# Heads' projection of a transformer layer: the turn by position moved from VectorE into each token's weights, keys and queries in the two row halves of TensorE's array

## What is computed

```python
h = _rmsnorm(x, ln1_w)
q = (h @ wq.T).reshape(Bx, Tx, NH, HD).transpose(0, 2, 1, 3)
k = (h @ wk.T).reshape(Bx, Tx, NKV, HD).transpose(0, 2, 1, 3)
v = (h @ wv.T).reshape(Bx, Tx, NKV, HD).transpose(0, 2, 1, 3)
q = q * cos + _rotate_half(q) * sin          # cos, sin: a row for each position
k = k * cos + _rotate_half(k) * sin
k, v = jnp.repeat(k, NREP, axis=1), jnp.repeat(v, NREP, axis=1)
scores = jnp.einsum('bhtd,bhsd->bhts', q, k) / jnp.sqrt(jnp.float32(HD))
```

## Time and profile before

| | |
|---|---|
| three runs | median 1144.41 us (1140.83 to 1145.59) |
| the profiled execution | 1143.9 us, its span in the trace 1142.1 us |
| mean granted TensorE clock | 0.965 of 2.4 GHz |
| busy share of the span: PE, PEld, DVE, ACT, POOL | 91%, 67%, 76%, 52%, 39% |
| heads' projection (project1) | 587.2 to 652.5 us |
| heads (heads1) after it | from 653.3 us |

### The profile page before, as it was taken

How to read it: one execution, slowest core, us unless ns; L and a number is a source line. 1 busy time by engine, 2 the same in 40 slices (tenths; PEclk the granted TensorE clock), 3 DMA queues, 4 the chain that set the end, 5 groups by cost and what they waited for, 6 DMA issues and landing times. The chain is left out here.

```text
span 1142.1 us, 24219 instructions
## 1 busy us (share of the span) xinstructions
PE 1038.3 (91%) x8559; PEld 765.1 (67%) x8559; DVE 865.5 (76%) x2076; ACT 598.7 (52%) x1293; POOL 449.5 (39%) x599
## 2 busy tenths in 40 slices
PE   6697868589999999998889899986999999999996
PEld 2376756467777777776765467764777777777775
DVE  1696969757777777778878689965788887787876
ACT  2275646465556555666334457764554545545542
POOL 3233402303444344434357377724133333333332
PEclk9798999889999999999899999997999999999999
DMA  8200000000000000000000000000000000000000
GB/s 231 119 1 1 3 1 2 1 1 2 1 2 1 2 1 1 1 1 1 1 1 1 1 1 3 3 2 0 2 6 7 7 7 13 7 6 7 7 7 13
DMA packets 3456, 13.59 MB, mean 12 GB/s; under 512 B 400, under 2 KB 2192, under 8 KB 2960
## 3 DMA queue, kind: packets, MB, share of 16 engines
q1 hardware_dynamic: 3056, 8.00, 2.5%
q0 software_dynamic: 288, 4.11, 0.9%
HBM read 9.98 MB, written 2.13 MB: 11 GB/s over the span
## 5 line engine op out<-in xcount | busy, mean ns | idle before, releaser
L1461 PE MATMUL moe_psU<-moe_nT_parts,moe_w_hi 128*128 128x320 f32 x988 | 325.0, 339 | 3.4 <-DVE moe_hid L1356 2.5
L1461 PE MATMUL moe_psU<-moe_nT_parts,moe_w_lo 128*128 128x320 f32 x988 | 297.0, 311 | 0.0
L1461 PEld LDWEIGHTS moe_psU<-moe_nT_parts,moe_w_hi 128*128 128x128 f32 x988 | 188.3, 191 | 58.4 <-issue 50.1
L1461 PEld LDWEIGHTS moe_psU<-moe_nT_parts,moe_w_lo 128*128 128x128 f32 x988 | 188.9, 191 | 0.0
L1350 DVE TENSOR_TENSOR moe_hid<-moe_psU,moe_silu 128x320 f32<-128x320 f32 x286 | 139.3, 491 | 57.6 <-ACT moe_silu L1123 49.3
L1033 POOL TENSOR_TENSOR moe_sum<-moe_scaled 128x256 f32<-128x256 f32 x124 | 94.9, 765 | 163.4 <-DVE moe_scaled L1340 163.2
L1123 ACT ACTIVATE moe_silu<-moe_psU 128x320 f32<-128x320 f32 x286 | 125.4, 438 | 57.3 <-PE moe_psU L1461 45.0
L1128 ACT ACTIVATE moe_hid<-moe_psU,middle 128x320 f32<-128x320 f32 x260 | 129.3, 526 | 32.1 <-PE moe_psU L1461 30.0
L1356 DVE TENSOR_SCALAR moe_hid<-moe_psU,middle 128x320 f32<-128x320 f32 x156 | 85.5, 549 | 56.5 <-PE moe_psU L1461 55.5
L1472 PE MATMUL moe_psY<-moe_hid,late 128*64 128x320 f32 x832 | 123.5, 439 | 0.8 <-DVE moe_hid L1350 0.8
L1472 PE MATMUL moe_psY<-moe_hid,middle 128*64 128x320 f32 x832 | 123.5, 439 | 0.7 <-ACT moe_hid L1128 0.7
(11 more groups left out here) (322 smaller groups left out, 1887.6 us busy)
## 6 DMA issues: line engine op xcount, KB each, us to landing
images<-in_x SPq DMA_DIRECT2D x8, 576.0 KB, 11.5
late<-in_late POOLq DMA_DIRECT2D x1, 2456.5 KB, 12.1
out_tokens<-h SPq DMA_DIRECT2D x13, 160.0 KB, 1.8
middle<-in_middle POOLq DMA_DIRECT2D x1, 1554.0 KB, 7.0
early<-in_early SPq DMA_DIRECT2D x1, 1043.0 KB, 19.2
early<-in_early SPq DMA_DIRECT2D x1, 80.0 KB, 2.0
```

The source lines that it names most:

```text
L1461: last = pe.matmul(psum[:, 0:HALF], w[:, col:col + SPLIT], moving, start=(part == 0), stop=(part == 1))
```

## The change

It leaves out `product`, `rotate` and `fold`, and with them VectorE's and GpSimd's part in keys and queries.

- A table "turns" (128 x 65 x 64 floats, 2.1 MB) holds for each position the 16 x 16 matrix that turns a head, once for each head, with 1/4 in those for the queries. Its first group is loaded in the tokenizer, after late; the others by SP in project1, into three buffers, each once the weights' product that used the buffer is done.
- `turned_weights(g)` is one product of 320 columns with wqk (128 x 128, keys in the upper half, queries in the lower), which gives each of the five tokens' own weights: rows 0 to 63 for keys, 64 to 127 for queries. ScalarE copies them (`weights`) into one of two turned_w buffers, 16 columns of every 32; the others are zeroed once by GpSimd.
- normalise writes each token twice, side by side, so that the transposes give nT in both row halves, 128 rows.
- `keys_and_queries(g)` on TensorE is ten products of 64 rows by 128 columns, five tokens in the upper row half into psK, and five in the lower into psQ, in turn. ScalarE copies psK and psQ into kx and qx.
- The values side has a PSUM bank of its own (psV); its ScalarE copy no longer waits for the next transposes.

TensorE's order is now keys and queries of g, values side of g, transposes of g + 1, weights of g + 1. The prediction calls these KQ, side, T and the weights' product. ScalarE's is transposed of g + 1, weights of g + 1, square of g + 3, keys and queries of g, sides of g.

```diff
+def twice_over(dve, dst, src, per_token):
+
+    shape = [B, T, 2, D]
+    return dve.tensor_tensor(dst[:, :, :].rearrange("b t (x d) -> b t x d", x=2), src[:, :, :].unsqueeze(2).to_broadcast(shape),
+                             per_token.unsqueeze(2).unsqueeze(3).to_broadcast(shape), ALU.mult)
...
+                pool.dma_start(turns_first[:, :, :], dram_turns[:, 0:T, :]).then_inc(late_in, 16)
...
-        n_tile, k_parts = [n_first, sb("n_tile1", [B, T, D])], [sb(f"k_parts{k}", [128, TOK]) for k in range(2)]
-        psT, psQ, psK, psF = ps("psT", 128, TOK), ps("psQ", 128, TOK), ps("psK", 128, TOK), ps("psF", 128, TOK)
...
+        n_tile = [n_first, sb("n_tile1", [B, T, 2 * D])]
+        turns = [turns_first] + [sb(f"turns{k}", [128, T, D]) for k in range(2)]
+        turned_w = [sb(f"turned_w{k}", [128, T, 128]) for k in range(2)]
+        psT, psQ, psK = ps("psT", 128, TOK), ps("psQ", 128, TOK), ps("psK", 128, TOK)
+        psW, psV = ps("psW", 128, T * D)[:, 0:T * D], ps("psV", 128, T * B // 4)[:, 0:T * B // 4]
...
+            @block.sync
+            def _(sp):
+                for g in range(1, NT):
+                    need(sp, W_mm, g - 2)
+                    sp.dma_start(turns[g % 3][:, :, :], turns_d[:, g * T:(g + 1) * T, :]).then_inc(turns_in[g % 3], 16)
+
             @block.gpsimd
             def _(pool):
                 pool.memset(halves[:, :], -0.5).then_inc(half_set, 1)
                 pool.wait_ge(half_set, 1)
+                for w in turned_w:
+                    pool.memset(w[:, :, :], 0.0).then_inc(blank, 1)
+                pool.wait_ge(blank, 2)
                 for g in range(NT):
-                    pool.memset(nT[D:, g * TOK:(g + 1) * TOK], 0.0).then_inc(blank, 1)
-                    pool.wait_ge(blank, g + 1)
...
-                    dve.tensor_tensor(n_tile[g % 2][:, :, :], cen[g % 3][:, :, :], over_width(stats[g % 3][:, 4, :]),
-                                      ALU.mult).then_inc(n_set, 1)
+                    twice_over(dve, n_tile[g % 2], cen[g % 3], stats[g % 3][:, 4, :]).then_inc(n_set, 1)
                     dve.tensor_tensor(x[:, g * T:(g + 1) * T, :], cen[g % 3][:, :, :], over_width(stats[g % 3][:, 3, :]),
                                       ALU.mult).then_inc(x_set, 1)
-
-                def rotate(src, table, g, dst):
-                    angles = late[:, c[table]][:, g * T:(g + 1) * T].unsqueeze(2).to_broadcast([128, T, B])
-                    return dve.tensor_tensor(dst.rearrange("p (t b) -> p t b", b=B),
-                                             src[:, 0:TOK].rearrange("p (t b) -> p t b", b=B), angles, ALU.mult)
-
-                def keys(g):
-                    dve.wait_ge(K_mm, g + 1)
-                    need(dve, F_mm, g - 1)
-                    rotate(psK, "ropek", g, k_parts[g % 2][:, :]).then_inc(k_parts_set, 1)
-
-                def queries(g):
-                    dve.wait_ge(Q_mm, g + 1)
-                    rotate(psQ, "ropeq", g, at(qx, g)).then_inc(q_set, 1)
 
...
                 for g in range(NT):
                     if g < NT - 3:
                         centre(g + 3)
-                    keys(g)
                     if g < NT - 2:
                         normalise(g + 2)
                     if g < NT - 3:
                         variance(g + 3)
-                    queries(g)
 
             @block.scalar
             def _(act):
@@ -1865,31 +1866,37 @@
 
                 def transposed(g):
                     act.wait_ge(T_mm, g + 1)
-                    act.activation(at(nT, g)[0:D, :], psT[0:D, 0:TOK], ACT.Copy, scale=late[0:D, c["ln1"]]).then_inc(nT_set, 1)
-
-                def folded(g):
-                    act.wait_ge(F_mm, g + 1)
-                    act.copy(at(kx, g), psF[:, 0:TOK]).then_inc(k_set, 1)
+                    act.activation(at(nT, g), psT[:, 0:TOK], ACT.Copy, scale=late[:, c["ln1"]]).then_inc(nT_set, 1)
+
+                def weights(g):
+                    act.wait_ge(W_mm, g + 1)
+                    act.wait_ge(blank, 2)
+                    need(act, Q_mm, g - 1)
+                    act.copy(turned_w[g % 2][:, :, :].rearrange("d t (h x i) -> d t h x i", h=NH, x=2)[:, :, :, 0, :],
+                             psW.rearrange("d (t h i) -> d t h i", t=T, h=NH)).then_inc(w_set, 1)
 
                 def keep_sides(g):
                     act.wait_ge(V_mm, g + 1)
-                    if g < NT - 1:
-                        act.wait_ge(T_mm, g + 2)
                     act.copy(sides[:, :, g * T:(g + 1) * T].rearrange("p q t -> p t q"),
-                             side_ps.rearrange("p (t q) -> p t q", t=T)).then_inc(side_set, 1)
-
+                             psV.rearrange("p (t q) -> p t q", t=T)).then_inc(side_set, 1)
+
+                def keys_and_queries(g):
+                    act.wait_ge(Q_mm, g + 1)
+                    act.copy(at(kx, g), psK[:, 0:TOK]).then_inc(k_set, 1)
+                    act.copy(at(qx, g), psQ[:, 0:TOK]).then_inc(q_set, 1)
+
+                transposed(0)
+                weights(0)
                 square(1)
-                transposed(0)
                 square(2)
                 for g in range(NT):
+                    if g < NT - 1:
+                        transposed(g + 1)
+                        weights(g + 1)
                     if g < NT - 3:
                         square(g + 3)
-                    if g < NT - 1:
-                        transposed(g + 1)
+                    keys_and_queries(g)
                     keep_sides(g)
-                    if g > 0:
-                        folded(g - 1)
-                folded(NT - 1)
 
...
-                        last = pe.transpose(psT[0:D, t * B:(t + 1) * B], n_tile[g % 2][:, t, :], early[:, ec["ident"]])
+                        last = pe.transpose(psT[:, t * B:(t + 1) * B], n_tile[g % 2][:, t, :], early[:, ec["ident"]])
                     last.then_inc(T_mm, 1)
 
-                def product(g, psum, w, read, done):
+                def turned_weights(g):
+                    need(pe, turns_in[g % 3], 16 * ((g + 2) // 3 if g % 3 else g // 3))
+                    need(pe, w_set, g)
+                    pe.matmul(psW, late[:, c["wqk"]], turns[g % 3][:, :, :].rearrange("k t m -> k (t m)"),
+                              start=True, stop=True).then_inc(W_mm, 1)
+
+                def keys_and_queries(g):
                     pe.wait_ge(nT_set, g + 1)
-                    pe.wait_ge(blank, g + 1)
-                    need(pe, read, g)
-                    for begin, n in pieces():
-                        last = pe.matmul(psum[:, begin:begin + n], late[:, c[w]], nT[:, g * TOK + begin:g * TOK + begin + n],
-                                         start=True, stop=True)
-                    last.then_inc(done, 1)
-
-                def fold(g):
-                    pe.wait_ge(k_parts_set, g + 1)
+                    pe.wait_ge(w_set, g + 1)
                     need(pe, k_set, g)
-                    for begin, n in pieces():
-                        last = pe.matmul(psF[:, begin:begin + n], late[:, c["fold"]], k_parts[g % 2][:, begin:begin + n],
-                                         start=True, stop=True)
-                    last.then_inc(F_mm, 1)
+                    need(pe, q_set, g)
+                    for t in range(T):
+                        col = g * TOK + t * B
+                        for rows, psum in ((slice(0, D), psK), (slice(D, 2 * D), psQ)):
+                            last = pe.matmul(psum[:, t * B:(t + 1) * B], turned_w[g % 2][rows, t, :], nT[rows, col:col + B], start=True, stop=True)
+                    last.then_inc(Q_mm, 1)
 
                 def values_side(g):
-                    pe.wait_ge(nT_set, g + 1)
                     need(pe, side_set, g)
                     tokens = at(nT, g).rearrange("p (t q j) -> p t q j", t=T, j=4)
                     for j in range(4):
-                        last = pe.matmul(side_ps[32 * j:32 * j + 32, :], late[:, c["wv"]], tokens[:, :, :, j], start=True, stop=True)
+                        last = pe.matmul(psV[32 * j:32 * j + 32, :], late[:, c["wv"]], tokens[:, :, :, j], start=True, stop=True)
                     last.then_inc(V_mm, 1)
 
                 transposes(0)
+                turned_weights(0)
                 for g in range(NT):
-                    product(g, psK, "wkx", k_parts_set, K_mm)
+                    keys_and_queries(g)
                     values_side(g)
                     if g < NT - 1:
                         transposes(g + 1)
-                    if g > 0:
-                        fold(g - 1)
-                    product(g, psQ, "wqx", q_set, Q_mm)
-                fold(NT - 1)
+                        turned_weights(g + 1)
...
+    own, swapped = np.eye(HD), np.eye(HD)[(np.arange(HD) + HD // 2) % HD]
+    one = own[:, None, :] * np.cos(emb).T[None] + swapped.T[:, None, :] * (np.sin(emb) * swap_sign).T[None]
+    turns = np.zeros((128, L, NH, HD))
+    for hd in range(NH):
```

(29 more changed lines are left out.)

25 lines of the change are left out of this document (13 added, 12 removed).

## The result

The changed kernel took 1169.2 us (median of four runs, 1165.6 to 1174.8), beside 1145.0 for four runs of the kernel before on the same chip: a ratio of 1.0218 (95% interval 1.0174 to 1.0262), 2.2% slower. One of the four runs before, 1161.5 us, was in a slower state, and such runs are left out of this and every later ratio. The range of 1146 to 1170 held the result by 0.8 us; the point of 1154 was 15 us too low. The profiled execution took 1170.72 us.

What follows compares the result with a forecast made beforehand. It took one series loop through TensorE and ScalarE, 5.50 us a group against 4.60, to bound the changed projection: 1143.9 + 7.1 (loop, start and end) + 3 (clock dips) = 1154.0 us, range 1146 to 1170.

Steps and rivals of the forecast that it cites:

- What becomes late: Heads' projection: ScalarE's copies of psK and psQ stand behind its work on g+1, putting everything in one series loop.
- The terms of the loop: Projection: KQ, side, transposes to ScalarE and ScalarE's five instructions sum to 5.50 us a group, against 4.60.
- TensorE's sum: Projection rival: TensorE's work, 4.60 falling to 3.2 us a group, decides; 18 us off, 1126; chance 0.07.
- Row halves: KQ's ten products: upper and lower row halves run side by side, so KQ takes 1.33 us, not 2.45.
- passes queue: Rival in KQ: halves take turns or loads wait, KQ 2.35 to 2.45 us, +13 to +15, 1164 to 1166; chance 0.06.
- Edits at nothing: VectorE's multiplications, GpSimd's memsets, turns loads and queue changes priced at nothing; an uncovered load at most 2 us, once.
- The clock: Projection: TensorE's clock dips to half in waits, near 1 us each; three taken, +3 us.
- always half: Projection at half clock throughout: +2.7 us a loop, 13 x 2.7 = +35 us.
- half clock most of the time: Rival: TensorE's clock in the projection is at half most of the time, 1165 to 1186 us; chance 0.12.
- The forecast proper: Whole kernel: the series loop plus a few clock dips, 1149 to 1162 us; chance 0.60.
- Slower: Whole kernel: time above 1150.1 us, beyond half a per cent (5.7 us); chance 0.72.

Runs made afterwards that it cites:

- e1_copies_first: Changed kernel with ScalarE's copies of keys and queries of g moved ahead of transposed and weights of g + 1; ratio 0.9942 to the kernel before.
- e2_ahead: Changed kernel with TensorE's transposes and weights' product of g + 1 issued before keys and queries of g; ratio 0.9927 to the kernel before.

## Why the prediction was right or wrong

- **What becomes late: right.** KQ waits for the queries' copy in every group, ScalarE's five instructions stand end to end, and either reorder that breaks this chain gives a kernel faster than before.
- **The terms of the loop: right, small errors.** With the clock full it is 5.60 us (5.50 forecast). From the timeline above: transposes to ScalarE 0.83 (0.77), transposed 0.70 (0.69), weights 0.30 (0.32), square 0.37 (0.37), keys 0.57 (0.59), queries to KQ's load 0.83 (0.74, the largest miss); KQ at full clock 1.32 (1.33). With the values side's 0.69 that is 5.61.
- **TensorE's sum: right.** 3.23 us where nothing else held it, for 3.2.
- **Row halves: right.** 1.32 against 2.08 apart. The "passes queue" rival of 2.35 to 2.45 would have been too dear even where it does happen.
- **Edits at nothing: right.** A turns load lands in 2.2 us and the weights' product waits for none.

The page's DMA issue row for it:

```profile
project_turns<-in_turns SPq DMA_DIRECT2D x8, 160.0 KB, 2.2
```

- **The clock: the step that failed.** "A dip as long as that row costs near 1 us; I take three: +3." The price was nearly right, 1.2 a loop. The count was eleven more than before's one, and the term 13.9 us. I placed the loop between two rows, busy 9.19 of 13.60 us at full clock and 3.50 of 6.70 followed by half, and took a value near the first for a loop that repeats. In this loop the dip came back in every turn. The "always half" bound, +2.7 a loop, was too high for what happened: it doubles KQ, the values side and the transposes and brings the weights' product out. KQ alone took the half clock in full (1.12 as reckoned), the values side kept its 0.70, and the transposes and the weights' product ran mostly at full clock.
- **The numbers.** Of the 26.8 us in the span, 9.0 are the series loop at full clock (forecast 7.1; the loop's 0.10 makes 1.1 of the difference, a half-clock stretch in the second loop 0.6), 13.9 the half clock (forecast 3), and about 4 lie ahead of the projection. It was the rival "half clock most of the time" (1165 to 1186), which had 0.12, at half for 50% of the stage; without the 4 the profiled execution would have taken about 1167, near the rival's lower edge. The forecast proper, 1149 to 1162, missed. That the range still held the median, by 0.8 us, was close to luck: it took in only the low end of that rival, and the profiled execution, 1170.72, lies outside it. "Slower", with 0.72, was right and for the right reason, the series; more than half of the loss has the other cause.

## What to carry to other kernels

When an edit takes work off TensorE, write down who must read each result before its buffer is free, and where that reader stands in its engine's order: TensorE lost 1.4 us a group here and the loop grew by 1.0 at full clock, while moving one line in ScalarE's program turned 2.2% slower into 0.6% faster. A loop in which TensorE waits in every turn must be priced with its clock for every turn, and not for a few. An instruction moved to another engine leaves the chain only if nothing ahead of it there waits for the chain.

## What the runs showed of the hardware that was not expected

- **A clock in step with the program.** 1.00 and 0.50 in turn, 3.4 us each, for ten loops. TensorE was busy 44.12 of 66.70 us there, for 13.21 of 22.00 in the kernel whose clock stayed at 1.00; the first share holds passes that the half clock itself had lengthened, so the two do not compare. Two idle products in the wait, 0.64 us of TensorE's time, kept the clock full and saved some 14 us of the projection.
- **Half clock did not slow the values side.** Its products of 160 columns in the four column quarters took 0.70 us in each of eleven groups at a granted clock of 0.50, and 0.69 at 1.00 before the change, while KQ went from 1.32 to 2.44. Why is open.
- **Half-clock stretches of the same code differ between executions**, and with them some 4 to 11 us. The changed kernel's tokenizer had one of 13.7 us where the kernel before had 3.4. Its first attention proper began at 104.80 us for 100.67, so the 4 us that the span lost outside the projection were lost by then. The one load more in the tokenizer is not the cause: in the profiles of e1_copies_first and e2_ahead, which have it too, the clock is 1.00 from 20.8 to 34.5 us. The window in the changed kernel:

```profile
20.80:34.50 13.70, 12.87 (x48) 4.57 (x49) 2.85 (x5) 2.13 (x4) 1.80 (x3) 0.50 0.82 299
```

  The first attention's combine stage, untouched in all, took 73.5 us at a clock of 0.98 in the kernel before, and 84.4 at 0.82 in another run's profile, here of the copies-first kernel:

```profile
148.60:233.00 84.40, 66.65 (x523) 47.56 (x523) 57.85 (x137) 39.14 (x148) 16.35 (x10) 0.82 0.00 1
```

  So a single span says less than a stage read by its own marks, which is why the table above compares projections.
- **Row halves are taken up out of the written order.** With the keys' products all ahead, the queries' first pass started beside the keys' eighth, and from there they ran in pairs until the keys were done.
